# The inverse of the gated delta rule: one level at a time, or one PSUM bank of a level at a time

## The reference, cut to what matters

```python
def step(S, inp):
    q_t, k_t, v_t, g_t, b_t = inp
    Sk = jnp.einsum('bhkv,bhk->bhv', S, k_t)
    delta = jnp.einsum('bhv,bhk->bhkv', v_t, k_t) - jnp.einsum('bhv,bhk->bhkv', Sk, k_t)
    S = jnp.exp(g_t)[..., None, None] * S + b_t[..., None, None] * delta
    o_t = jnp.einsum('bhkv,bhk->bhv', S, q_t)
    return (S, o_t)
```

## Time and profile before

| what | value |
|---|---|
| median of 3 runs | 4140.53 us (4137.81 to 4141.64) |
| the profiled execution, its own time | 4146.86 us |
| span of the profiled execution | 4143.2 us |
| PE busy | 3800.3 us (92%) |
| DVE busy | 3129.4 us (76%) |
| ACT busy | 2403.0 us (58%) |
| POOL busy | 1088.0 us (26%) |

### The profile page before, as it was taken

One profiled execution on the slowest core, in us unless ns is written; L12 is line 12 of the kernel. 1 busy time (PEld: TensorE's weight loads), 2 busy tenths in 40 slices (PEclk: granted clock), 3 DMA queues, 4 the chain that ended last, 5 costly groups with the idle time before them and its releaser, 6 DMA issues. The chain is left out here.

```text
span 4143.2 us, 110709 instructions
## 1 busy us (share of the span) xinstructions
PE 3800.3 (92%) x43533; PEld 2237.9 (54%) x43533; DVE 3129.4 (76%) x5127; ACT 2403.0 (58%) x3581; POOL 1088.0 (26%) x1044
## 2 busy tenths in 40 slices
PE   5999968888889888996869999999999999999998
PEld 4444358777788777675653444444444444444443
DVE  5799957777777775447968887878787887878786
ACT  2788846666666664253443665656565565656564
POOL 1000056666666663007763000000000000000000
PEclk9999979999999999998987999999999999999999
DMA  3544442322322222253442000000000000000000
GB/s 129 180 126 128 126 130 91 98 94 93 98 92 96 94 91 68 82 158 105 108 112 52 10 10 15 4 19 5 20 3 10 15 10 13 5 20 5 8 15 10
DMA packets 271735, 264.18 MB, mean 64 GB/s; under 512 B 53760, under 2 KB 232064, under 8 KB 270496
## 3 DMA queue, kind: packets, MB, share of 16 engines
q1 hardware_dynamic: 250768, 226.07, 18.2%
q0 software_dynamic: 6144, 16.79, 1.2%
q10 hardware_dynamic: 14352, 14.55, 1.0%
HBM read 151.95 MB, written 105.38 MB: 62 GB/s over the span
## 5 line engine op out<-in xcount | busy, mean ns | idle before, releaser
L2456 DVE TENSOR_REDUCE part_max<-p_m 128x1 f32<-128x512 f32 x2118 | 1362.9, 685 | 379.3 <-PE p_m L2298 371.8
L2438 ACT ACTIVATE prob<-p_s 128x1024 f32<-128x1024 f32 x1024 | 1047.7, 1023 | 749.0 <-PE p_s L2362 747.0
L2317 PE MATMUL p_o<-prob,v_one 128*64 128x512 f32 x4096 | 1055.4, 592 | 3.9 <-ACT prob L2438 0.5
L2298 PE MATMUL p_m<-keys,queries 96*64 96x512 f16 x4236 | 661.7, 387 | 28.0 <-DMA keys<-parts_d 20.4
L2362 PE MATMUL p_s<-queries,keys 97*64 97x512 f16 x4096 | 619.3, 380 | 0.0
L916 PE MATMUL pd_both<-both,step 64*64 64x128 f32 x8192 | 504.5, 273 | 67.7 <-issue 35.6
L2362 PEld LDWEIGHTS p_s<-queries,keys 97*64 97x64 f16 x4096 | 228.9, 109 | 598.2 <-issue 592.7
L916 PEld LDWEIGHTS pd_both<-both,step 64*64 64x64 f32 x8192 | 458.3, 134 | 95.8 <-issue 78.5
L2266 POOL TENSOR_TENSOR attn<-o_num,o_inv 32x512 f32<-32x512 f32 x64 | 80.9, 1264 | 1458.5 <-DVE o_inv L2475 1452.0
L2298 PEld LDWEIGHTS p_m<-keys,queries 96*64 96x64 f16 x4236 | 239.1, 108 | 310.0 <-DVE part_max L2456 56.3
L2317 PEld LDWEIGHTS p_o<-prob,v_one 128*64 128x64 f32 x4096 | 288.5, 136 | 162.4 <-issue 15.8
(11 more groups left out here) (242 smaller groups left out, 5722.8 us busy)
## 6 DMA issues: line engine op xcount, KB each, us to landing
q_d<-conv_q SPq DMA_DIRECT2D x16, 1024.0 KB, 5.0
v_d<-conv_v SPq DMA_DIRECT2D x16, 1024.0 KB, 5.1
k_d<-conv_k SPq DMA_DIRECT2D x16, 1024.0 KB, 6.5
sums<-sums_d SPq DMA_DIRECT2D x128, 128.0 KB, 3.1
kq_t<-k_d SPq DMA_DIRECT2D x32, 512.0 KB, 3.7
kq_t<-q_d SPq DMA_DIRECT2D x32, 512.0 KB, 5.2
sums_k<-sums_d SPq DMA_DIRECT2D x128, 128.0 KB
v_t<-v_d SPq DMA_DIRECT2D x32, 512.0 KB
```

Source lines behind the costliest of these rows:

```text
L2298: last = te.matmul(p_m[k % 2][x * HALF:(x + 1) * HALF, :], queries[0:ROW, p, hh, at:at + HALF], keys[0:ROW, 2 * p + hh, kb * BLK:(kb + 1) ...
L2317: product = te.matmul(p_o[64 * hh:64 * hh + VW, :], g.v_one[:, j, p, hh:hh + 2, :].rearrange("p a d -> p (a d)"), prob[:, j % 2, hh, :], s ...
L2438: a.activation(prob[:, j % 2], p_s[j % 2][:], ACT.Exp, scale=SCORE_SCALE).then_inc(exp_d, 1)
L2456: v.tensor_reduce(part_max[:, hh * SUB + sub, kb:kb + 1], p_m[k % 2][:], AX.X, ALU.max).then_inc(red_d, 1)
```

## The change

Each level is done in two halves by PSUM bank, pairs 0 to 3 (low) and then pairs 4 to 7 (high), on all three engines, with semaphores of its own for the low half. PE waits for the low half of `step` and `both`, makes the low products (with the short products between them, as before), then waits for the high half and makes the high products. DVE does `turn_low`, `mask_low`, `turn_high`, `mask_high` where it did `turn` and `mask`. ACT makes two copies where it made one, in `keep_factor` and `keep_both`. `starts` signals twice. Level 5, `keep_half`, `last_step` and `keep_inverse` stay whole. The waits of a short product now stand ahead of the level's low half. In DVE's order `take_rows(pre, 0)` now comes ahead of the whole of level (1, 4), where it stood between its turn and its mask. For each couple DVE has 4 instructions where it had 2 for each of levels 1 to 4 of both x: 16 more; ACT has 8 more; PE has the same products in the same order.

```diff
+        def wait_low(n, x, k):
             if k == 1:
                 pe.wait_ge(inv1_d[x], n.now)
-            if k < NL:
-                pe.wait_ge(step_d[x], n.masked[k])
-            else:
-                pe.wait_ge(last_d[x], n.now)
+            pe.wait_ge(low_step_d[x], n.masked[k])
+            pe.wait_ge(low_up_d[x], n.masked[k])
+
+        def wait_high(n, x, k):
+            pe.wait_ge(step_d[x], n.masked[k])
             pe.wait_ge(up_d[x], n.made[k])
...
+        def part(b, long, short=None):
+            last = None
+            for p in range(HALF):
+                for h in range(2):
+                    a = long(b * HALF + p, h)
+                    if short is not None:
+                        for hh in range(2):
+                            last = short(2 * p + h, hh)
+            return a, last
+
         def starts(n, x):
             wait_start(n, x)
-            over_heads(start_factor(n, x)).then_inc(upmm_d[x], 1)
+            part(0, start_factor(n, x))[0].then_inc(low_mm_d[x], 1)
+            part(1, start_factor(n, x))[0].then_inc(upmm_d[x], 1)
...
+        def doubles(n, x, k, short=None):
+            wait_low(n, x, k)
+            made, beside = part(0, double(n, x, k), short)
+            if k < NL - 1:
+                made.then_inc(low_mm_d[x], 1)
+            wait_high(n, x, k)
+            part(1, double(n, x, k))[0].then_inc(upmm_d[x], 1)
+            return beside
...
         def keep_both(n, x, k):
+            act.wait_ge(low_turn_d[x], n.masked[k + 1])
+            a.activation(both[x][:, bank(0), :], p_both[x][:, bank(0), :], ACT.Copy).then_inc(low_up_d[x], 1)
             act.wait_ge(turn_d[x], n.level[k + 1])
-            a.activation(both[x][:], p_both[x][:], ACT.Copy).then_inc(up_d[x], 1)
+            a.activation(both[x][:, bank(1), :], p_both[x][:, bank(1), :], ACT.Copy).then_inc(up_d[x], 1)
...
+        def turn_low(n, x, k):
+            dve.wait_ge(low_mm_d[x], n.masked[k])
+            if k == 1:
+                dve.wait_ge(last_d[x], n.last)
+            v.transpose(turned[x][:, bank(0), :], p_both[x][:, bank(0), 0:C]).then_inc(low_turn_d[x], 1)
+
+        def mask_low(n, x, k):
+            dve.wait_ge(low_turn_d[x], n.masked[k])
+            v.tensor_tensor(step[x][:, bank(0), :], turned[x][:, bank(0), :], over_half(masks[:, k - 1, :]), ALU.mult).then_inc(low_step_d[x], 1)
+
+        def turn_high(n, x, k):
+            dve.wait_ge(upmm_d[x], n.made[k])
+            v.transpose(turned[x][:, bank(1), :], p_both[x][:, bank(1), 0:C]).then_inc(turn_d[x], 1)
+
+        def mask_high(n, x, k):
+            dve.wait_ge(turn_d[x], n.level[k])
+            v.tensor_tensor(step[x][:, bank(1), :], turned[x][:, bank(1), :], over_half(masks[:, k - 1, :]), ALU.mult).then_inc(step_d[x], 1)
+
+        def level(n, x, k):
+            turn_low(n, x, k)
+            mask_low(n, x, k)
+            turn_high(n, x, k)
+            mask_high(n, x, k)
...
             if pre is not None:
-                turn(pre, 1, 4)
                 take_rows(pre, 0)
-                mask(pre, 1, 4)
+                level(pre, 1, 4)
```

More of the change, by code:

```diff
@@ L748, in phase_delta @@
     first_d, turn_d, step_d, last_d, upmm_d, up_d = (sem2(s) for s in ("first", "turn", "step", "last", "upmm", "up"))
+    low_turn_d, low_step_d, low_mm_d, low_up_d = (sem2(s) for s in ("low_turn", "low_step", "low_mm", "low_up"))
     g.used_sems = sems
@@ L755, in over_pairs, with over_half, bank @@
         return spread(ap.unsqueeze(1), W)
+    def over_half(ap):
+        return spread(ap.unsqueeze(1), [P, NPAIR // 2, C])
     B32 = C // 2
     SAME, OTHER = range(2)
+    HALF = NPAIR // 2
+    def bank(b):
+        return slice(b * HALF, (b + 1) * HALF)
     def blocks_of(h):
@@ L905, in wait_double @@
         def wait_double(n, x, k):
+            pe.wait_ge(last_d[x], n.now)
+            pe.wait_ge(up_d[x], n.made[k])
+        def wait_low(n, x, k):
             if k == 1:
                 pe.wait_ge(inv1_d[x], n.now)
-            if k < NL:
-                pe.wait_ge(step_d[x], n.masked[k])
-            else:
-                pe.wait_ge(last_d[x], n.now)
+            pe.wait_ge(low_step_d[x], n.masked[k])
+            pe.wait_ge(low_up_d[x], n.masked[k])
+        def wait_high(n, x, k):
+            pe.wait_ge(step_d[x], n.masked[k])
             pe.wait_ge(up_d[x], n.made[k])
@@ L1005, in long_beside_short @@
             return a, b
+        def part(b, long, short=None):
[7 more added lines that the diff above has]
+            return a, last
         def starts(n, x):
             wait_start(n, x)
-            over_heads(start_factor(n, x)).then_inc(upmm_d[x], 1)
-        def doubles(n, x, k):
-            wait_double(n, x, k)
-            over_heads(double(n, x, k)).then_inc(upmm_d[x], 1)
+            part(0, start_factor(n, x))[0].then_inc(low_mm_d[x], 1)
[8 more added lines that the diff above has]
+            return beside
         def inverse_alone(n, ahead):
@@ L1064, in together @@
             doubles(pre, 0, 1)
-            wait_double(pre, 1, 1)
             wait_key_rows(post, 1)
[L1067 to L1071, removed]
+            doubles(pre, 1, 1, key_rows(post, 1)).then_inc(kr_d[1], 1)
             wait_new(post, 0, pre)
[L1073 to L1076, removed]
+            doubles(pre, 0, 2, new_state(post, 0)).then_inc(new_d, 1)
             wait_outputs(post, 0)
[L1078 to L1082, removed]
+            doubles(pre, 1, 2, new_outputs(post, 0)).then_inc(o_d, 1)
             wait_residual(post, 1, pre)
[L1084 to L1087, removed]
+            doubles(pre, 0, 3, residual(post, 1)).then_inc(res_d, 1)
             wait_key_rows(pre, 0)
-            made, turned_keys = long_beside_short(double(pre, 1, 3), key_rows(pre, 0))
-            made.then_inc(upmm_d[1], 1)
-            turned_keys.then_inc(kr_d[0], 1)
+            doubles(pre, 1, 3, key_rows(pre, 0)).then_inc(kr_d[0], 1)
             wait_updates(post, 1)
@@ L1100, in together @@
             new.then_inc(new_d, 1)
-            wait_double(pre, 1, 4)
             wait_outputs(post, 1)
-            made, out = long_beside_short(double(pre, 1, 4), new_outputs(post, 1))
-            made.then_inc(upmm_d[1], 1)
-            out.then_inc(o_d, 1)
+            doubles(pre, 1, 4, new_outputs(post, 1)).then_inc(o_d, 1)
             for x in range(2):
@@ L1162, in keep_factor @@
         def keep_factor(n, x):
+            act.wait_ge(low_turn_d[x], n.masked[1])
+            a.activation(both[x][:, bank(0), 0:C], p_both[x][:, bank(0), 0:C], ACT.Copy).then_inc(low_up_d[x], 1)
             act.wait_ge(turn_d[x], n.level[1])
-            a.activation(both[x][:, :, 0:C], p_both[x][:, :, 0:C], ACT.Copy).then_inc(up_d[x], 1)
+            a.activation(both[x][:, bank(1), 0:C], p_both[x][:, bank(1), 0:C], ACT.Copy).then_inc(up_d[x], 1)
         def keep_both(n, x, k):
+            act.wait_ge(low_turn_d[x], n.masked[k + 1])
+            a.activation(both[x][:, bank(0), :], p_both[x][:, bank(0), :], ACT.Copy).then_inc(low_up_d[x], 1)
             act.wait_ge(turn_d[x], n.level[k + 1])
-            a.activation(both[x][:], p_both[x][:], ACT.Copy).then_inc(up_d[x], 1)
+            a.activation(both[x][:, bank(1), :], p_both[x][:, bank(1), :], ACT.Copy).then_inc(up_d[x], 1)
         def keep_half(n, x):
@@ L1285, in turn_first @@
             v.transpose(inv_low[x][:], both[x][:, :, C:2 * C]).then_inc(first_d[x], 1)
+        def turn_low(n, x, k):
[17 more added lines that the diff above has]
+            mask_high(n, x, k)
         def turn(n, x, k):
             dve.wait_ge(upmm_d[x], n.made[k])
-            if k == 1:
-                dve.wait_ge(last_d[x], n.last)
             v.transpose(turned[x][:], p_both[x][:, :, 0:C]).then_inc(turn_d[x], 1)
-        def mask(n, x, k):
-            dve.wait_ge(turn_d[x], n.level[k])
-            v.tensor_tensor(step[x][:], turned[x][:], over_pairs(masks[:, k - 1, :]), ALU.mult).then_inc(step_d[x], 1)
         def one(post, pre, ahead):
@@ L1301, in one @@
                 turn_first(pre, 1)
-                turn(pre, 0, 1)
-                mask(pre, 0, 1)
+                level(pre, 0, 1)
             if post is not None:
@@ L1306, in one @@
             if pre is not None:
-                turn(pre, 1, 1)
-                mask(pre, 1, 1)
+                level(pre, 1, 1)
             if pre is not None:
-                turn(pre, 0, 2)
-                mask(pre, 0, 2)
+                level(pre, 0, 2)
                 if post is not None:
                     take_rows(post, 1)
[L1314 to L1317, removed]
+                level(pre, 1, 2)
+                level(pre, 0, 3)
             if post is not None:
@@ L1322, in one @@
             if pre is not None:
[L1323 to L1326, removed]
+                level(pre, 1, 3)
+                level(pre, 0, 4)
             if post is not None:
```

## The result

The changed kernel takes 4209.85 us (median; 4204.94 to 4215.21) where the kernel before takes 4139.17: a ratio of 1.0171 (95% interval 1.0157 to 1.0185), 70.7 us slower. The forecast was 4147, no change, with a range of 4106 to 4190.

A forecast was written before the change was run, and what follows sets the result against it. DVE was taken to bound the stretch from residual 0 to residual 1, PE the rest; -3.4 + 5.8 + 4 + 0.9 - 1 = +6.3 us on the median of 4140.5 gave 4147, range 4106 to 4190.

The forecast's parts named there:

- The cut at the residuals: Each iteration divided at DVE's residuals: first part from residual 0 to 1 (532.9 us), second to the next residual 0 (502.5).
- DVE without gaps: The forecast's mechanism: DVE works almost without idle time between residual 0 and residual 1; chance 0.65.
- second part: From residual 1 to the next residual 0: bounded by PE, busy 93%; change counted as +0.9 us in all.
- the fixed part: DVE's added cost of splitting a level's turn and mask: 0.24 us a level, 1.68 per first part.
- The +5.8: Between the residuals: 0.2 us of new DVE idle on each of 29 iterations, an estimate.
- the +4 given back: In the two longest stretches DVE was idle over 4 us; only half of that was given back, +4 us.
- that excess: The mean mask's time above 0.69 us, longer beside POOL: 0.27 us a level, taken as unchanged by halving.
- rival B: Each half mask waits for POOL as the whole did: +58.6 us, 4205; sign, pairs above 1.2 us; chance 0.13.
- Rival A: PE is the bound; its 54.6 us of waits on DVE go, median 4086, or 4113 with half; chance 0.14.
- PE's wait for the mask before level (1,1) nearly gone: Profile sign: level (1,1) starts on its low half about 1 us earlier, so the 22.4 us of mask waits shrink.
- the state: Ahead of level 3 of x = 0: the new state comes late, PE waiting about 1 us an iteration for it.
- C: PE pauses between halves of levels (0,4) and (1,4) in the second part: 12.4 us, 4159; chance 0.08.

The follow-up runs named there:

- mask_first_late: mask_first_bank with the early start taken away: PE waits for both halves and ACT copies whole; 4122.4 us, ratio 0.9963.
- mask_first_bank: The changed kernel with turn and mask exchanged: DVE multiplies from PSUM by a turned mask, then turns the product SBUF to SBUF, in halves; 4099.3 us, ratio 0.9907.
- mask_first_whole: The kernel before, levels whole, with turn and mask exchanged (multiply from PSUM by a turned mask, then turn); 4105.7 us, ratio 0.9936.

## Why the prediction was wrong

**Right: what bounds.** The cut at the residuals, 88% of DVE in the first part, and "DVE without gaps" after. DVE has no idle time over 0.15 us there now. The second part kept its length.

**Nearly right: the fixed part.** The half turn was taken as 0.433 between bounds of 0.354 and 0.708; it is 0.433 to 0.439. A level whose masks don't wait now steps by 1.63 us (the median of 64), where it took 1.36 before (35 levels):

```profile
1301.13 0.43 DVE L1307 STREAM_TRANSPOSE turned<-pd_both 128x256 f32<-128x256 f32 x1
...
1302.76 0.44 DVE L1307 STREAM_TRANSPOSE turned<-pd_both 128x256 f32<-128x256 f32 x1
```

So it costs 0.27 more by itself and not 0.24: 59 us in 217 levels, and not 52. That about fills the 55.5 us that DVE had idle. The +5.8 for new idle time of DVE and the +4 given back did not come: DVE has 0.49 us without work in a stretch, which is 14 steps from a half turn to its mask of 0.035 us each.

**Wrong: "I leave that excess, 0.27 a level, unchanged, since the same columns are read and written".** That is the step that failed. The excess does not go with columns. It is the rest of a POOL instruction, paid by each mask that comes on one. By the prediction's own terms a pair of half masks carries 1.37 - 0.83 = 0.54 us of it, twice 0.27; counted between the residuals it is 127.2 / 217 = 0.59. With twice 0.27 the sum is 0.27 x 217 = +58.6 on 4147, so 4205, against 4209.85 measured. That is rival B with its price, to which I gave 0.13, and the sign named for B came: pairs of half masks above 1.2 us. B's picture, that each half waits as the whole did, holds on the mean alone: fewer of the halves wait (49% against 67%), each for longer. That these two nearly cancel was not foreseen. Nor is it all merit that the sum comes so close: the 7 us too little for the fixed part and the 10 too little for the excess (68.9 in place of 58.6) stand against the 9.8 us of idle time that did not come. The row of its opposite was on the page: of the masks in one iteration some took 0.69 and one 1.48. One subtraction, 1160.28 - 1159.73, would have hinted at where the mask ends, and the same for a few more masks would have shown it.

**Rival A's mechanism: right in another kernel, not seen in this one.** Against mask_first_late the early start is worth 18 us between the residuals. In the changed kernel PE's waits did not shrink, since DVE had no time left.

**Wrong: "PE's wait for the mask before level (1,1) nearly gone".** Waits for the low half of the mask are 23.6 us, where those for the whole mask were 22.4; in the iteration shown the one before level (1,1) is 0.81 us. There the low half comes late, at 1297.79: it waited for POOL itself, as the two half masks of level (0,1) ahead of it had.

**Right, but not the largest: the state.** I expected PE to wait about 1 us for it in each iteration; it is 0.86 in the iteration shown, and 29.3 us of "issue" ahead of levels fit that. More of the wait, 65.1 us, stands at the residual. In that iteration two levels of DVE's list come behind the state, and their four half masks of 1.09, 0.94, 1.38 and 0.79 us meet a row of POOL instructions that runs nearly without a pause.

**C** didn't happen: the second part did not grow.

## What to carry to other kernels

Split an instruction to start its consumer earlier only after counting what each piece has to wait for: where a wait lasts until a whole instruction of another engine has ended, each piece can meet it (here 251 halves did, where 171 whole masks had). Here the cure was to let one operand come from PSUM, by exchanging an elementwise product and a blockwise transpose, which commute once the mask is transposed too; that was worth 28 us to the kernel before and 110 to the changed one. Average busy shares (DVE 72%) would have hidden the part of the loop where the engine was at 88%.

## What the runs showed of the hardware that was not expected

A mask that starts beside a POOL arithmetic instruction ends a constant behind it: 0.28 us for 256 columns, 0.55 for 512, which is its own time less 0.14 in both. Such a mask shows in the trace as long and not as idle time. POOL is held up as well: in the kernel before `q_g` takes 1.18 us, but 1.64 in the 30 cases where a whole mask is under way as it starts; with half masks that is 1.37, and in mask_first_bank all 64 take about 1.19. POOL's indirect DMA `slots_d<-rows,place` delays no mask (62 masks started beside one in the changed kernel). A transpose from SBUF to SBUF is free of it: 0.445 us for 256 columns and 0.709 for 512, on the mean, the same beside POOL as alone.

PE's pause ahead of the updates is longer now (2.18 us in the iteration shown, where it was 1.20), and the granted clock was below 0.95 in 13 of the 31 second parts, where it was in 1 before. Two of them, the first at full clock, the other partly at the lower one of the two (1.2 in place of 2.4 GHz), with 0.90 granted on the mean:

```profile
1311.44:1326.50 15.06, 14.81 (x414) 13.17 (x416) 9.29 (x18) 11.48 (x25) 9.58 (x10) 1.00 0.33 109
...
1381.18:1397.57 16.39, 16.23 (x414) 14.80 (x416) 9.29 (x17) 11.49 (x25) 9.61 (x10) 0.90 0.33 101
...
sum 501.98, PE 482.07 PEld 430.56 DVE 285.20 ACT 362.43 POOL 291.42; mean PE 15.55 PEld 13.89 DVE 9.20 ACT 11.69 POOL 9.40
```

The same 414 matmuls keep PE busy for 1.4 us longer. That the pause is the cause was not tried. PE's busy time in the second parts rose from 467.2 to 482.1 us, though their length did not, because PE had less idle time in them, 19.9 us against 35.3. In mask_first_bank that idle time is 516.5 - 476.4 = 40.1, much of it in pauses that the profile puts down to no engine ("issue"), and some of the gain is given back there: the first parts are 59 us shorter than before, the span 44 (4143.2 to 4099.2). It does not come with any shorter first part, as in mask_first_whole the second parts take 500.9. What these pauses are was not tried, and as "issue" can hide a wait for an engine, none is ruled out.
